# Selective scan in two halves: the second half started from a kept state instead of a carry product

## What is computed

```
# B = 2 samples, L = 1024 time steps, D_INNER = 512 channels, D_STATE = 16 states
dA = jnp.exp(dt_t[..., None] * A)
h  = dA * h + (dt_t * x_t)[..., None] * B_t[:, None, :]
y  = jnp.einsum('bdn,bn->bd', h, C_t)
```

## Time and profile before

| | us |
|---|---|
| median of 3 runs | 670.87 (670.55 to 675.84) |
| the profiled execution | 671.71 |
| its span, first to last instruction | 669.5 |
| first scan starts (DVE, L1603) | 119.29 |
| last multiplication by C ends (POOL, L557) | 452.85 |
| PE busy over the span | 620.7 |
| DVE busy | 525.9 |
| ACT busy | 386.0 |
| POOL busy | 363.4 |

### The profile page before, as it was taken

One profiled execution on the slowest core, in us unless ns is written; L12 is line 12 of the kernel. 1 busy time (PEld: TensorE's weight loads), 2 busy tenths in 40 slices (PEclk: granted clock), 3 DMA queues, 4 the chain that ended last, 5 costly groups with the idle time before them and its releaser, 6 DMA issues.

```text
span 669.5 us, 26260 instructions
## 1 busy us (share of the span) xinstructions
PE 620.7 (93%) x11916; PEld 447.6 (67%) x11916; DVE 525.9 (79%) x489; ACT 386.0 (58%) x783; POOL 363.4 (54%) x132
## 2 busy tenths in 40 slices
PE   2999999899998999899999999999899699999997
PEld 1443445788887898777998789988655355555533
DVE  5895711889988998799899998986978697992465
ACT  1774785998775777588778677521155345333100
POOL 1000514499987998789899988890300044533000
PEclk9998999999998999999999999999799799999999
DMA  7990645200263202412340100016058899790203
GB/s 224 76 83 4 179 138 169 57 20 20 65 161 70 82 20 50 129 52 69 113 112 21 51 21 20 4 36 195 1 118 183 174 245 211 179 175 1 59 6 125
DMA packets 72630, 62.17 MB, mean 93 GB/s; under 512 B 34024, under 2 KB 57576, under 8 KB 72520
## 3 DMA queue, kind: packets, MB, share of 16 engines
q1 hardware_dynamic: 71560, 60.09, 40.2%
q10 hardware_dynamic: 960, 0.41, 0.2%
HBM read 44.22 MB, written 15.25 MB: 89 GB/s over the span
## 4 chain that ended last, share of the span: by engine, by line
PE 78%; ACT 6%; DMA 6%; DVE 5%; issue 4%; SPq 1%; DVEq 0%; ACTq 0%
PE PS L1139 31%; PE PS L1161 8%; PE PS L1019 7%; PE PS L1276 7%; DMA patch_rows<-arena 5%; PE PS L1367 4%; PE PS L1189 4%; PE PS L1382 4%; PE PS L1158 2%; DVE X L1603 1%; PE PS L990 1%; PE PS L1255 1%; ACT arena L793 1%; SPq L483 1%; PE PS L1353 1%
## 5 line engine op out<-in xcount | busy, mean ns | idle before, releaser
L557 POOL TENSOR_TENSOR X<-X,spare 128x2048 f32<-128x2048 f32 x32 | 146.8, 4587 | 18.7 <-DVE X L1603 9.3
L1139 PE MATMUL PS<-mid,arena 128*32 128x128 f32 x4096 | 137.2, 273 | 8.1 <-issue 6.6
L1139 PEld LDWEIGHTS PS<-mid,arena 128*32 128x32 f32 x4096 | 122.2, 110 | 19.9 <-issue 13.2
L1139 PE MATMUL PS<-WPR,arena 128*32 128x128 f32 x2048 | 130.4, 275 | 4.8 <-DVE X L1603 2.9
L1139 PE MATMUL PS<-APROD,arena 128*32 128x128 f32 x2048 | 129.6, 275 | 3.5 <-issue 3.3
L1139 PEld LDWEIGHTS PS<-WPR,arena 128*32 128x32 f32 x2048 | 112.5, 111 | 17.0 <-issue 9.6
L1139 PEld LDWEIGHTS PS<-APROD,arena 128*32 128x32 f32 x2048 | 111.8, 111 | 2.5 <-issue 2.2
L793 ACT ACTIVATE arena<-arena,small 128x512 f32<-128x512 f32 (+1 forms) x150 | 99.3, 711 | 20.0 <-DVE X L1603 9.3
L557 POOL TENSOR_TENSOR arena<-arena,spare 128x2048 f32<-128x2048 f32 x16 | 73.4, 4589 | 12.8 <-DVE arena L1603 6.9
L582 POOL TENSOR_TENSOR arena<-arena,PWR 128x512 f32<-128x512 f32 x30 | 40.6, 1380 | 72.5 <-PE PS L1276 72.4
L557 POOL TENSOR_TENSOR WIN<-WIN,spare 128x2048 f32<-128x2048 f32 x16 | 73.4, 4590 | 7.8 <-DVE WIN L1603 6.4
(11 more groups left out here) (186 smaller groups left out, 1067.3 us busy)
## 6 DMA issues: line engine op xcount, KB each, us to landing
arena<-dt_rows SPq DMA_DIRECT2D x56, 256.0 KB, 4.0
arena<-patch_rows SPq DMA_DIRECT2D x40, 324.0 KB, 6.2
patch_rows<-arena SPq DMA_DIRECT2D x10, 648.0 KB, 7.6
X<-in_x SPq DMA_DIRECT2D x4, 1024.0 KB, 7.2
dt_rows<-arena SPq DMA_DIRECT2D x8, 512.0 KB, 3.2
spare<-c_rows SPq DMA_DIRECT2D x64, 64.0 KB, 2.2
tap_rows<-WPR SPq DMA_DIRECT2D x24, 88.0 KB, 8.2
mid<-dt_rows SPq DMA_DIRECT2D x8, 256.0 KB, 3.4
```

The source lines that it names most:

```text
L557: pool.tensor_tensor(HB[s % 4], HB[s % 4], CROW[:, k % 2:k % 2 + 1, :].broadcast_to([P, QN, HALF]), ALU.mult).then_inc(S["g_rd"], 1)
L1139: mm = pe.matmul(PS[32 * n:32 * n + 32, 4 + i, j * P:(j + 1) * P], DXT[:, DT_ * b + g, 4 * h + j, 32 * i:32 * i + 32], DIAGB[k % 2][n][:, ...
```

## The change

In second halves each part is scanned by two instructions of 512 columns, each with its own kept state as initial value. The carry product and all that served it is gone: `half_way`, `middle_column` (L1571), `carry`, the one-column matmuls and two thirds of what `late_by_four` laid out (the rates of sample 1 remain, `late_rates_by_four`). In second halves `decay` writes both tiles in full (128x512). The kept column is copied by POOL in front of its multiplication, not by ACT. Before sample 1 begins, DVE clears the first column of the three DECAY buffers again (`clear_first`). Two waits on `col_rd` become waits on `top_rd`.

```diff
             def late_by_four():      # now late_rates_by_four
-                pe.wait_ge(S["a0_rd"], NG)
+                pe.wait_ge(S["rate_rd"], B)
...
@@ gpsimd, loop over s
                 pool.wait_ge(S["scan_rd"], 2 * s + 2)
                 if h == 0:
+                    pool.tensor_copy(CARRY[:, DT_ * b + g, nq, :], HB[s % 4][:, :, HALF - 1]).then_inc(S["kept"], 1)
                     pool.wait_ge(S["kept"], NQ * DT_ * b + DT_ * nq + g + 1)
...
@@ scalar
-            def half_way(e):
-                b, g = divmod(e, DT_)
-                act.wait_ge(S["rate_rd"], b + 1)
-                act.wait_ge(S["col_rd"], b + 1)
-                act.activation(LATE[:, 1 + b, g, :], rates_of(b)[:, g, :], ACT.Exp, scale=DTMAX[:, e:e + 1]).then_inc(S["a0_rd"], 1)
...
                 for i in (2 * p, 2 * p + 1):
-                    at, first = (i - 2 * p) * HALF, i % 2
+                    at, first = (i - 2 * p) * HALF, 0 if h else i % 2
...
-            for e in range(NG):
-                half_way(e)
             diagonals(1, 2)
-            keep_last(1)
             decay(6)
...
             for s in range(DT_, STEPS):
                 k, g = divmod(s, DT_)
-                keep_last(s - 2)
                 decay(2 * s)
-                if s == DT_ + 1:
-                    take_halves()
+                if s == DT_:
+                    take_late_rates()
...
@@ tensor, inputs(s, p)
-                if h:
-                    pe.wait_ge(S["carry_rd"], NQ * b + nq + 1)
...
                             mm = pe.matmul(PS[32 * n:32 * n + 32, 4 + i, j * P:(j + 1) * P], DXT[:, DT_ * b + g, 4 * h + j, 32 * i:32 * i + 32],
-                                           DIAGB[k % 2][n][:, j, :], start=True, stop=not (h and j == 0 and i % 2))
-                        if h and j == 0 and i % 2:
-                            for n in range(QN):
-                                pe.matmul(PS[32 * n:32 * n + 32, 4 + i, 0:1], IDENT[:, 32 * n:32 * n + 32], CARRY[:, DT_ * b + g, nq, i:i + 1], start=False, stop=True)
+                                           DIAGB[k % 2][n][:, j, :], start=True, stop=True)
...
@@ vector, scan(s, p)
-                start = CARRY[:, DT_ * b + g, nq, 2 * p:2 * p + 1] if h else 0.0
...
+                if h:
+                    dve.wait_ge(S["kept"], NQ * DT_ * b + DT_ * nq + g + 1)
+                    first, second = (CARRY[:, DT_ * b + g, nq, 2 * p + r:2 * p + r + 1] for r in range(2))
+                    dve.tensor_tensor_scan(HB[s % 4][:, 2 * p, :], DECAY[q % 3][:, 0:HALF], bank(2 + p, 0), first, ALU.mult, ALU.add)
+                    dve.tensor_tensor_scan(HB[s % 4][:, 2 * p + 1, :], DECAY[q % 3][:, HALF:], bank(2 + p, 1), second, ALU.mult, ALU.add).then_inc(S["scan_rd"], 1)
+                else:
+                    if b and p + 2 * nq * DT_ + 2 * g < 3:
+                        dve.wait_ge(S["zero_again"], p + 2 * g + 1)
+                    dve.tensor_tensor_scan(...as before..., 0.0, ALU.mult, ALU.add).then_inc(S["scan_rd"], 1)
+
+            def clear_first(q):
+                dve.wait_ge(S["scan_rd"], q - 2)
+                dve.memset(DECAY[q % 3][:, HALF:HALF + 1], 0.0).then_inc(S["zero_again"], 1)
```

More of the change, by code:

```diff
@@ L149, in mamba_attention_kernel @@
         RATES = view(small, 256, DT_, NS)
-        LATE = small[:, 320:512].rearrange("p (k g n) -> p k g n", k=3, g=DT_)
+        RATES1 = view(small, 320, DT_, NS)
         RATEQ = view(small, 512, QN, DT_, NQ)
-        LATEQ = small[:, 576:768].rearrange("p (i k g q) -> p i k g q", i=QN, k=3, g=DT_)
+        RATEQ1 = view(small, 576, QN, DT_, NQ)
         SELQ = sb("SELQ", [P, 2, 32])
@@ L341, in rates_of @@
         def rates_of(b):
-            return LATE[:, 0] if b else RATES
+            return RATES1 if b else RATES
         def rates_at(b):
-            return LATEQ[:, :, 0] if b else RATEQ
+            return RATEQ1 if b else RATEQ
         @block.sync
@@ L701, in take_dxt, with take_late_rates @@
                     act.wait_ge(dt_st[e - DT_], 16)
-                    act.wait_ge(S["col_rd"], 1)
+                    act.wait_ge(S["top_rd"], DT_)
                 act.activation(DXT[:, e].rearrange("p j c -> p (j c)"), tile_pair("tr", e), ACT.Copy).then_inc(S["dxt_rd"], 1)
-            def half_way(e):
-                b, g = divmod(e, DT_)
-                act.wait_ge(S["rate_rd"], b + 1)
-                act.wait_ge(S["col_rd"], b + 1)
-                act.activation(LATE[:, 1 + b, g, :], rates_of(b)[:, g, :], ACT.Exp, scale=DTMAX[:, e:e + 1]).then_inc(S["a0_rd"], 1)
-            def take_halves():
+            def take_late_rates():
                 act.wait_ge(S["quad_ps"], 2)
-                act.activation(LATEQ.rearrange("p i k g q -> p (i k g q)"), bank(pair_of("halves", 0), 0)[:, 0:3 * QN * NS], ACT.Copy).then_inc(S["quad_rd"], 1)
+                act.activation(RATEQ1.rearrange("p i g q -> p (i g q)"), bank(pair_of("halves", 0), 0)[:, 0:QN * NS], ACT.Copy).then_inc(S["quad_rd"], 1)
             def diagonals(k, n):
@@ L1064, in rates_by_four, with late_rates_by_four @@
                 mm.then_inc(S["quad_ps"], 1)
-            def late_by_four():
+            def late_rates_by_four():
                 pe.wait_ge(*freed("halves", 0))
-                pe.wait_ge(S["a0_rd"], NG)
+                pe.wait_ge(S["rate_rd"], B)
                 for i in range(QN):
                     for n in range(QN):
-                        to = bank(pair_of("halves", 0), 0)[32 * n:32 * n + 32, 48 * i:48 * i + 48].rearrange("p (g n) -> p g n", n=QN)
-                        mm = pe.matmul(to, IDENT[:, 32 * i:32 * i + 32], LATE.rearrange("p k g (q n) -> p (k g) n q", n=QN)[:, :, n, :], start=True, stop=True)
+                        to = bank(pair_of("halves", 0), 0)[32 * n:32 * n + 32, NS * i:NS * i + NS].rearrange("p (g n) -> p g n", g=DT_)
+                        mm = pe.matmul(to, IDENT[:, 32 * i:32 * i + 32], RATES1.rearrange("p g (q n) -> p g n q", n=QN)[:, :, n, :], start=True, stop=True)
                 mm.then_inc(S["quad_ps"], 1)
@@ L1175, in _ @@
                     inputs(s, c)
-                    if s == DT_ and c:
-                        late_by_four()
+                    if s == DT_ and c == 0:
+                        late_rates_by_four()
                     if s >= 3 - c:
@@ L1602, in scan @@
                 dve.wait_ge(S["u_ps"], q + 1)
-                dve.tensor_tensor_scan(HB[s % 4][:, 2 * p:2 * p + 2, :].rearrange("p g l -> p (g l)"), DECAY[q % 3], pair(2 + p), start, ALU.mult, ALU.add).then_inc(S["scan_rd"], 1)
-            def carry(b, nq):
-                part = CARRY[:, DT_ * b:DT_ * b + DT_, nq, 1::2]
-                dve.wait_ge(S["quad_rd"], 2)
-                dve.wait_ge(S["kept"], NQ * DT_ * b + DT_ * nq + DT_)
-                dve.tensor_tensor(part, part, LATEQ[:, 1::2, 1 + b, :, nq].rearrange("p i g -> p g i"), ALU.mult).then_inc(S["carry_rd"], 1)
+                if h:
[6 more added lines that the diff above has]
+                        dve.wait_ge(S["zero_again"], p + 2 * g + 1)
+                    dve.tensor_tensor_scan(HB[s % 4][:, 2 * p:2 * p + 2, :].rearrange("p g l -> p (g l)"), DECAY[q % 3], pair(2 + p), 0.0, ALU.mult, ALU.add).then_inc(S["scan_rd"], 1)
+            def clear_first(q):
+                dve.wait_ge(S["scan_rd"], q - 2)
+                dve.memset(DECAY[q % 3][:, HALF:HALF + 1], 0.0).then_inc(S["zero_again"], 1)
             def gate(s):
@@ L1620, in _ @@
                 scan(s, 0)
+                if s == STEPS // 2 - 1:
+                    clear_first(STEPS)
+                elif s == STEPS // 2:
+                    clear_first(STEPS + 2)
                 scan(s, 1)
-                b, h, nq, _g = step_of(s - 3)
-                if s >= 3 and h == 0 and s % DT_ == 2:
-                    carry(b, nq)
+                if s == STEPS // 2 - 1:
+                    clear_first(STEPS + 1)
                 if s >= 3 and step_of(s - 3)[2] == NQ - 1:
```

19 lines of the change are left out of this document (4 added, 15 removed).

## The result

| | us |
|---|---|
| before, median of 20 runs | 672.85 (667.38 to 679.88) |
| changed, median of 20 runs | 665.81 (662.92 to 671.67) |
| ratio, with its 95% interval | 0.9902 [0.9885, 0.9919] |
| forecast beside the median of before | 667.6 (662.5 to 673.5) |

The change saves 1.0%, 6.6 us by the ratio, twice the 3.3 us of the forecast. The forecast of 667.6 was written beside a median of 670.87 from three runs; over 20 runs the kernel before is 2.0 us slower. That the measured 665.81 lies only 1.8 us from 667.6 is in part due to this: beside the new median the same gain of 3.3 us would have read 669.6, still with the result inside the range. The profiled execution of the changed kernel happens to be the slowest of its 20 (671.67 us, span 669.9), so the same kernel was profiled again beside the experiments (a1_again: 665.54 us, span 663.7).

What follows compares the result with a forecast made beforehand. PE, DVE and POOL were taken to lie within 6% of each other in the loop, PE busiest. Terms -2.0 + 0.5 - 2.4 + 1.0 - 0.4 = -3.3 us gave 667.6 beside a median of 670.87, range 662.5 to 673.5.

Steps and rivals of the forecast that it cites:

- Part 1: Loop start, first half of sample 0: a shorter ACT stream lets step 4 start earlier, 2.0 us gained (1.0 to 3.3).
- Part 2: First halves, 32 steps: POOL's kept-column copy and its wait lengthen POOL's step, 0.5 us lost (0 to 2.4).
- Part 3: Second halves, 64 parts: each added scan costs DVE 0.12 us (0.06 to 0.2), making its step 4.76 us.
- The +1.0 us of the gate stages: Stages 4 and 12, DVE the bound: gate steps go from 5.10 to 5.34 us, 1.0 us lost.
- Part 4: Second halves: dropping 64 sets of one-column matmuls frees 3.8 to 10.9 us of PE's stream.
- The term of stages 5, 6, 13 and 14: Second halves, nq = 1 and 2, 16 steps: PE's step falls to 4.79 us, 2.4 us gained, at most 4.9.
- the stalls of PE will not go: Stages 5, 6, 13 and 14: PE's stalls remain, and with DVE at 4.76 no engine could catch up.
- the term of the last groups: Stages 7 and 15, nq = 3: 0.6 us gained in stage 15, 0.2 lost in all, 0.4 gained.
- Rival 3: PE's issue stalls shrink with fewer instructions, and a matmul set costs 0.17 us: 662 us, chance 0.15.
- Rival 1: Second halves: DVE takes PE's place as bound, 672.7 us at 0.20 us a scan, chance 0.15.
- Rival 2: First halves: POOL becomes the bound through a copy priced like 192 elements, 674.1 us, chance 0.10.
- Rival 4: The change moves nothing: POOL eats the gain at the start before stage 3, 669.7 to 671 us, chance 0.15.

Runs made afterwards that it cites:

- a1_again: The changed kernel run and profiled once more, nothing altered: median 662.95 us, ratio 0.9911 to the kernel before.
- a3: The changed kernel with eight Exps of 128x16, read by nobody, back on ACT ahead of the diagonals: 661.13 us, ratio 0.9891 to the kernel before.
- b3: The kernel before with only the kept-column copy moved from ACT to POOL: 670.71 us, ratio 0.9969 to the kernel before.
- b1: The kernel before with only each second-half scan split into two of 512 columns, carry product kept: 673.46 us, ratio 1.0028.
- a4: The changed kernel with the 256 one-column matmuls back in second halves, adding the undecayed kept state: 670.40 us, ratio 1.0010 to the kernel before.
- b2: The kernel before with only the 256 one-column matmuls left out, carry products and waits kept: 663.50 us, ratio 0.9873.
- a7: The changed kernel with two one-element DVE copies ahead of each pair of scans, 128 in all: 668.01 us, ratio 0.9949 to the kernel before.

## Why the prediction was half right

**Part 1, the start (-2.0 forecast).** The step failed that ACT is what the rest waits for there and that its 1.68 us come back. ACT was late for two reasons at once: the Exps in front of the diagonals, and the copies that POOL waits for, far back in its stream. Only the second held up the end. a3 shows the first worth nothing; PE started step 4 at 136.20 instead of 136.37, not at 135. Stage 0 did move by -1.8 us, near the -2.0 forecast, but through part 2: that agreement is luck.

**Part 2, the copy on POOL (+0.5 forecast).** The price was too low, 0.26 us a step and not 0.20 (copy 0.20, wait 0.08, against 0.10 and 0.08), which puts POOL at 4.81, above PE's 4.79. But the sign was wrong too: I had written that POOL would wait for its own copy and not for ACT, and put no number on it. It is 1.8 us at the start (b3: 21.52 to 19.70 in stage 0), more than is given back behind it; b3 is 2.1 us faster than before. Parts 1 and 2 together were forecast at -1.5; first halves moved by -0.3 us by the stages of a1, and the single runs cannot resolve a difference of 1 us.

**Part 3, two scans for one (0.12 us each).** The price was near: 0.08 to 0.10 against 0.12. The Trainium skill (VectorE: DVE Perf Modes, section The TRN2 errata) gives 120 fixed cycles at 0.96 GHz for a PSUM source, by which I estimate 0.125 us. These scans, which follow each other, paid less than that for the cut. The +1.0 us of the gate stages did not come: stage 12 took 20.63 us and 20.68 before, since its gate steps went from 5.10 to 5.28 and PE's stalls covered that. In the kernel before the split costs 1.9 us, as b1 shows.

**Part 4, the one-column matmuls (-3.0 forecast: -2.4, and -0.6 in stage 15).** This is where the missing half is. The term of stages 5, 6, 13 and 14 was right in size (-2.4, measured -1.9). Wrong was the sentence that the stalls of PE will not go, and with it the term of the last groups: stages 7 and 15, from which I expected 0.4 us, gave 3.6. Nothing in the change addresses the stalls, I had written; but the waits are for packets of PE's instructions, and the change takes four of 94 away. PE's price of 4.36 at nq = 3 was wrong as well, since the lagging sums make it 4.79 in the first steps of these stages. Columns alone are worth 6.6 to 8.5 us (a4, b2): at most 2.9 of pace, 2.8 to 3.9 of waits for issue in the windows, the rest not assigned.

**Rival 3** had this mechanism and put it at 662 with a chance of 0.15; what came lies between it and the forecast. Its sign was to be the waits of the weight loads, and that was the wrong row. They are 24.4 us in b2, which is 8.5 us faster than before with 25.0, and 24.6 in a3, the fastest profile of all (span 659.8), against 31.5 in a1 (663.7). The weight loads' waits, in the first profile of the changed kernel and in a1_again:

```profile
PEld PS L1119 <- issue: 35.9, 69, 3.2
```

```profile
PEld PS L1119 <- issue: 31.5, 63, 2.5
```

These totals include waits under which matmuls still ran. PE's own idle time follows the time better: over the loop its waits for issue are 12.1 us in the first profile of the changed kernel, 8.6 in a1 and 6.5 in a3. I had said that I would be wrong if these waits changed by more than 5 us; they did, and it meant little.

**Rivals 1, 2 and 4.** DVE did not become the bound (0.08 to 0.10 against the 0.17 from which it decides), but a7 shows that it is near: 0.24 us more a step cost 3 us. POOL did, narrowly, by 0.02 us a step over PE at nq = 1 and 2. Rival 4, the gain at the start eaten by POOL, held for first halves (-0.3 us) and not for second ones.

What stays open: why four packets of instructions less, of 94, shorten the waits for them by about 3 us. Which packets come late, and whether it matters where their ends fall against the loads of dt, no run varied. Matmuls and their weight loads were not separated either, nor the place of the columns in a part, and some 2 us of the gain of a4 and b2 are neither in the pace nor in the waits counted here.
